# State-space layer and the end of a cross-attention, reordered by halves

## The chip, the cores and the metric

The kernel runs as one program on one core of a Trainium2 chip. The metric is the device time of an execution in microseconds (us). A profile is one execution, recorded instruction by instruction. In it PE is TensorE's matrix multiplication and PEld its weight loads, DVE is VectorE, ACT is ScalarE, POOL is GpSimd and SP issues most transfers. All work of this layer is in 32-bit floating point; the profile records one such matrix product as two MATMUL records and two LDWEIGHTS records, or one of each where the product is a transpose.

## The reference, cut to what matters

Two layers of attention, then feed-forward, work on 128 tokens (two sequences of 64) of width 256. The change lies in the second layer's cross-attention and in the state-space layer behind it.

```
# cross-attention: 16 heads of 16 channels over 1024 context keys and 64 own keys
attn = softmax(einsum('bhnd,bhmd->bhnm', q * scale, k)); out = einsum('bhnm,bhmd->bhnd', attn, v)
x = x + (out.reshape(B, N, C) @ w_proj.T + b_proj)

# state-space layer on xn = rmsnorm(layernorm(x)) * norm_w
z, xBC, dt = split(xn @ in_w.T)                       # 512, 768 and 8 columns
xBC = silu(causal_conv(xBC, conv_w, 4 taps) + conv_b) # per channel
xs, Bm, Cm = xBC[..., :512], xBC[..., 512:640], xBC[..., 640:]
dt = softplus(dt + dt_bias); A = -exp(A_log)
h = h * exp(dt*A) + (dt * xs) (x) Bm;  y = h . Cm     # step over 64 tokens, 8 heads
y = y + D * xs
y = rmsnorm(y * silu(z)) * gnorm_w
out = y @ out_w.T
```

The recurrence is computed as a masked product: for each head, the 128x128 matrix (Cm . Bm) * exp(cumulated dt*A difference) times dt * xs.

## The kernel before

Each engine has its own instruction list, written out by hand, and engines wait for one another by semaphores. `made(name)` is the value of a semaphore at which a named result is there, `tick(name)` the increment at the instruction that makes it; `ONCE` lists them in order. `step(ins)` makes DVE wait for its own instruction. `stay_warm(n, times)` puts 128x128 products of the identity, whose result nobody reads, into PE's list. PSUM has eight banks of 512 columns; `bank(n)` is one, `W[n]` two.

**Cross-attention's end.** A loop over 16 rows (a pair of heads of one sequence each) has PE make scores, DVE their maximum (L1160), ACT the exponentials with sums, PE transposes and products with the values (`attend1`, L1824). DVE copies four rows' products at a time from bank 6 (L1155); the last copy of 512 columns comes after the last row. DVE inverts all 16 sums, spreads them (L1187), PE spreads them over channels (L1840), PE gathers the heads into channel tiles (32 products of 64 columns, L1849), DVE multiplies 256 columns (L1191), PE projects (two products of 256 columns, L1855), DVE adds to x (L1194), normalises, and PE turns xn over (`turn_x`), which ACT copies to `xT` (L612).

**State-space layer.** Channels lie on partitions, tokens in columns: six tiles `CHT` of xBC (four of xs, then B and C). PE makes all six tiles (12 products, L1871), the step size dt (L1875) and z (L1879). DVE and ACT copy xBC to `XP` in SBUF; ACT applies the last tap and the bias for all tiles (L840), DVE the other three taps (18 instructions, L1222). Between the second and third of these rounds stand DVE's three instructions on dt (L1229 to L1231), for which PE's decay products wait (L1893, 8 of them, and L1895 for the sums). Then one tanh over all 768 columns (L847), one product by DVE (L1235), B times C and the transposes of xs (L1898, L1900), DTX and MT over all heads (L1240, L1245), PE's 8 products with them (L1906), DVE's four instructions on y, of 512 columns each (L1253 to L1255 with the D and norm-weight ones ahead), PE's output product (L1912) and sum of squares (L1917), DVE's variance (L1258), POOL's power and DVE's xn (L1260).

Of the kernel before, what the change touches and what calls it, by code (L numbers as in the profile page):

```python
# [6 lines left out]
ALU = mybir.AluOpType  # L7
# [22 lines left out]
CHT = CONV // P  # L30
PAD = NQ + TAPS - 1
# [89 lines left out]
SELF_BANK = ((4, 7), (5, 6))  # L121

# [89 lines left out]
def cut(base, at, *free):  # L212
# [5 lines left out]
    if len(free) == 1:  # L218
# [9 lines left out]
        "q1_ps", "k1_ps", "v1_ps", "rb_ps", "o1T_ps", "out1_ps", "xbc_ps", "dt_ps", "z_ps", "decay_ps", "G_ps",  # L228
        "xs_ps", "ym_ps", "y_tok_ps", "ssq_ps", "sc_ps", "pq_ps", "km_ps", "vm_ps", "lg_ps",
        "scT_ps", "rank_ps", "pmT_ps", "retT_ps", "ret_ps", "gate_ps", "route_ps", "maskT_ps"],  # L230
    "scalar_made": [
        "sqk_ready", "qr_sb", "sqq_ready", "qTA_sb", "kTA_sb", "simA_exp", "ptA_sb", "gT_sb", "xat_dup", "k1_sb", "rb_sb", "expA", "xbc_sbA", "dte",
        "dtl", "z_tanh", "conv_tanh", "cums", "ex_ready", "gm_ready", "ysq_ready", "pq_sb", "sct", "km_sb",
        "vm_sb", "pm_exp", "pmT_sb", "retT_sb", "gate_tanh", "hn_hi", "rz", "maskT_sb"],
    "vector_made": [
        "null_sb", "nv_ready", "kn_ready", "simA_max", "probsA", "hm_ready", "gT_lo", "rsel_ready", "o1_ready", "xbc_sbV",
        "dtn_ready", "dtA_ready", "conv_done", "xs_act", "M_ready", "yg_ready", "ya_ready", "scz", "scb_ready",
# [4 lines left out]
def perceiver_kernel(nc, x_in, ctx_in, ctxT_in, units_in, const_in, cols_in, vecs_in, rows_in, gate_in, out):  # L242
    with ExitStack() as stack:
# [161 lines left out]
        RSEL, RB, OT1 = cut(work, 0, ROWT, 32), cut(work, 512, KT, TOK), cut(work, 768, KT, TOK)  # L405
        probs1 = cut(pbuf, 0, 4, 1152)

        XP, C1 = cut(scr, 0, CHT, B, PAD), cut(scr, 832, CHT, TOK)
        XC, TH = cut(scr, 1600, CHT, TOK), cut(scr, 2368, CHT * TOK)
        ZS, ZT, ZW = cut(scr, 3136, DIN), cut(scr, 3648, DIN), cut(scr, 4160, DIN)  # L410
        DTX, Y2, GM = cut(scr, 4672, DIN), cut(scr, 5184, DIN), cut(scr, 5696, TOK)
        DX = cut(scr, 0, DIN)
        EX, MT = cut(pbuf, 0, NH, TOK), cut(pbuf, 1024, NH, TOK)
        YA, YGT, YSQ = cut(pbuf, 2048, DIN), cut(pbuf, 2560, 4, TOK), cut(scr, 3648, DIN)
# [106 lines left out]
        def _(pool):  # L521
# [23 lines left out]
            for n in range(N_RSQRT):  # L545
# [34 lines left out]
                if n == 6:  # L580
# [9 lines left out]
                    for n, (raw, (lo, hi)) in enumerate(((work, BIAS1), (xn, BIAS2))):  # L590
# [6 lines left out]
                        pool.wait_ge(ev("rows2_split"), n + 1)  # L597
                if n == 7:

                    pool.memset(XP[:, :, :, 0:TAPS - 1], 0.0).then_inc(ev("xp_zero"), 1)  # L600
# [5 lines left out]
        def _(act):  # L606
# [218 lines left out]
            act.wait_ge(*made("rb_ps"))  # L825
            act.copy(RB, bank(1)[:, 0:DIM].rearrange("p (i t) -> p i t", i=KT)).then_inc(*tick("rb_sb"))


            act.activation(expA, v_("A_log"), ACT.Exp).then_inc(*tick("expA"))
# [69 lines left out]
        def _(dve):  # L899
# [317 lines left out]
            for k in range(TAPS - 1):  # L1217
                for t in range(CHT):
                    if k == 0:
                        dve.wait_ge(ev("tap3"), t + 1)  # L1220
# [872 lines left out]
```

## Time and profile before

| | |
|---|---|
| time, median of 3 runs | 482.88 us (482.57 to 483.1) |
| the profiled execution | 483.39 us, span 481.5 us |
| PE busy | 460.1 us of the span, 3634 records |
| DVE, ACT, POOL busy | 263.4, 239.4, 124.5 us |
| granted TensorE clock | 1.000 over the span |
| state-space layer, first product to variance | 384.19 to 405.85 us |

The span runs from the first to the last instruction; the profiled execution's own time lies 1.89 us above it. PE's busy share says little in these two stages, since the identity products count as busy. What releases DVE, ACT and PE at each hand-over is read from the instructions in order of time.

### The profile page before, as it was taken

Reading aid. Unit: us, or ns where it says so; the run is one execution under the profiler, and the core shown is the slowest. Engines: PE = TensorE matmul, PEld = TensorE weight load, DVE = VectorE, ACT = ScalarE, POOL = GpSimd, SP = SyncE. Lnnn points to the kernel's source line nnn. Section 1 sums busy time; section 2 is a strip of 40 time slices with the busy share of each in tenths; the row PEclk is TensorE's granted clock in tenths of the full one; section 3 lists DMA queues with packets and bytes.
Section 4 is the critical chain, followed back from the end, with each engine's and each line's share of the span. In section 5 each row is a group of like instructions: output and inputs, shape, how many; then the busy total and the mean of one; then the engine's idle time right before and its main releaser. Section 6 shows DMA issues by size and latency. Waiting matters only on the chain.

```text
span 481.5 us, 8769 instructions
## 1 busy us (share of the span) xinstructions
PE 460.1 (96%) x3634; PEld 396.0 (82%) x3634; DVE 263.4 (55%) x461; ACT 239.4 (50%) x427; POOL 124.5 (26%) x114
## 2 busy tenths in 40 slices
PE   8999899999999999999978989999999899889997
PEld 7887989899997989899955769996666798778797
DVE  2666223255436231312256898956667465369996
ACT  2567233263535324222035877737888261237772
POOL 1110000002002300000020767969300000008795
PEclk9999999999999999999999999999999999999999
DMA  7925400006100020000079999991000093165000
GB/s 287 385 68 212 175 2 1 1 0 206 58 0 4 10 88 0 2 1 1 0 320 386 338 292 420 389 421 64 2 1 2 12 416 110 78 253 184 0 1 12
DMA packets 13191, 62.66 MB, mean 130 GB/s; under 512 B 1365, under 2 KB 3813, under 8 KB 7392
## 3 DMA queue, kind: packets, MB, share of 16 engines
q1 hardware_dynamic: 11072, 54.31, 29.8%
q0 software_dynamic: 2080, 7.80, 4.6%
q8 instruction: 29, 0.48, 0.4%
q14 instruction: 10, 0.08, 0.1%
HBM read 61.97 MB, written 0.13 MB: 129 GB/s over the span
## 4 chain that ended last, share of the span: by engine, by line
PE 73%; DVE 12%; POOL 6%; ACT 5%; issue 3%; DMA 1%; SPq 0%; DVEq 0%; ACTq 0%; POOLq 0%
PE W L1479 19%; PE W L1435 15%; POOL w_lo L541 5%; PE W L1638 5%; PE W L1708 4%; PE W L1762 3%; PE W L1807 3%; DVE w_lo L942 3%; PE W L1452 3%; PE W L1824 2%; PE W L1358 2%; PE W L1501 2%; DVE acts L1112 2%; PE W L1664 1%; PE W L1387 1%
## 5 line engine op out<-in xcount | busy, mean ns | idle before, releaser
L1479 PE MATMUL W<-probs_turned_hi,ctx_split_hi 128*128 128x256 f32 x256 | 72.9, 285 | 2.5 <-issue 2.5
L1479 PE MATMUL W<-probs_turned_hi,ctx_split_lo 128*128 128x256 f32 x256 | 72.5, 283 | 0.0
L1479 PE MATMUL W<-probs_turned_lo,ctx_split_hi 128*128 128x256 f32 x256 | 72.4, 283 | 0.0
L979 DVE TENSOR_TENSOR probs_turned_lo<-W,probs_turned_hi 128x512 fp32r<-128x512 f32 x32 | 20.6, 687 | 64.9 <-ACT probs_turned_hi L678 64.9
L550 POOL TENSOR_TENSOR small<-small,const 128x1 f32<-128x1 f32 (+2 forms) x10 | 6.9, 691 | 177.4 <-DVE small L1052 75.3
L1479 PEld LDWEIGHTS W<-probs_turned_hi,ctx_split_hi 128*128 128x128 f32 x256 | 49.1, 192 | 3.8 <-issue 3.3
L541 POOL TENSOR_TENSOR w_lo<-arena,w_hi 128x320 fp32r<-128x320 f32 x32 | 43.9, 1386 | 29.2 <-ACT w_hi L619 29.1
L1479 PEld LDWEIGHTS W<-probs_turned_lo,ctx_split_hi 128*128 128x128 f32 x256 | 49.1, 192 | 0.2
L1479 PEld LDWEIGHTS W<-probs_turned_hi,ctx_split_lo 128*128 128x128 f32 x256 | 49.1, 192 | 0.0
L942 DVE TENSOR_TENSOR w_lo<-arena,w_hi 128x704 fp32r<-128x704 f32 (+1 forms) x36 | 44.8, 1280 | 6.0 <-ACT w_hi L619 5.6
L697 ACT ACTIVATE pbuf<-W,small 128x1024 f32<-128x1024 f32 x16 | 17.9, 1117 | 59.6 <-DVE small L999 59.6
L541 POOL TENSOR_TENSOR w_lo<-ctxmem,w_hi 128x320 fp32r<-128x320 f32 (+1 forms) x30 | 46.7, 1579 | 1.9 <-ACT w_hi L619 1.5
L1708 PE MATMUL W<-w_hi,acts 128*128 128x256 f32 x240 | 44.2, 286 | 0.0
L619 ACT CAST w_hi<-arena 128x1024 fp32r<-128x1024 f32 x36 | 37.6, 1050 | 10.5 <-PE W L1638 6.1
L1435 PE MATMUL W<-ctx_turned_hi,q_keys_hi 128*128 128x512 f32 x128 | 41.0, 402 | 0.5 <-DVE q_keys_lo L972 0.5
L1435 PE MATMUL W<-ctx_turned_lo,q_keys_hi 128*128 128x512 f32 x128 | 39.7, 391 | 0.0
L1435 PE MATMUL W<-ctx_turned_hi,q_keys_lo 128*128 128x512 f32 x128 | 39.6, 390 | 0.0
L1708 PEld LDWEIGHTS W<-w_hi,acts 128*128 128x128 f32 x240 | 38.3, 191 | 0.1
L1638 PE MATMUL W<-w_hi,acts 128*128 128x512 f32 x112 | 36.4, 398 | 1.4 <-issue 1.3
L1358 PE MATMUL W<-const 128*128 128x128 f32 x290 | 36.6, 281 | 0.5 <-ACT xT L612 0.5
L1358 PEld LDWEIGHTS W<-const 128*128 128x128 f32 x290 | 34.7, 195 | 2.0 <-ACT xT L612 0.9
L689 ACT COPY scr<-W 128x256 f32<-128x256 f32 x32 | 11.8, 368 | 48.9 <-PE W L1479 48.9
(387 smaller groups left out, 923.0 us busy)
## 6 DMA issues: line engine op xcount, KB each, us to landing
arena<-units_dram SPq DMA_DIRECT2D x22, 1024.0 KB, 11.5
ctxmem<-units_dram SPq DMA_DIRECT2D x16, 1024.0 KB, 13.8
fixed<-units_dram SPq DMA_DIRECT2D x6, 1024.0 KB, 6.1
pbuf<-ctx_dram POOLq DMA_DIRECT2D x4, 512.0 KB, 5.2
ctxmem<-ctxT_dram SPq DMA_DIRECT2D x8, 256.0 KB, 11.3
ctxmem<-ctx_dram SPq DMA_DIRECT2D x2, 1024.0 KB, 14.5
scr<-ctx_dram POOLq DMA_DIRECT2D x3, 512.0 KB, 4.4
vecs<-vectors_dram POOLq DMA_DIRECT2D x1, 1040.0 KB, 7.6
```

What stands on the lines that cost most here:

```text
L541: pool.tensor_tensor(w_slot(1, p)[:, lo:hi], half_in(p)[:, lo:hi], f32(w_slot(0, p)[:, lo:hi]), ALU.subtract).then_inc(ev("lo_by_gpsimd"), 1)
L619: act.copy(w_slot(0, p), half_in(p)).then_inc(ev(hi_done(p)[0]), 1)
L697: act.activation(probs0[:, r % 2, :], W[r % 2][:, :], ACT.Exp, bias=negm[:, r:r + 1], accum_out=stat[:, r, 1:2]).then_inc(ev("exp_done"), 1)
L942: dve.tensor_tensor(w_slot(1, p)[:, lo:hi], half_in(p)[:, lo:hi], f32(w_slot(0, p)[:, lo:hi]), ALU.subtract).then_inc(ev("lo_by_vector"), 1)
L979: dve.tensor_tensor(PT[1][at], bank(4 + c).rearrange("p (t m) -> p t m", t=4), f32(PT[0][at]), ALU.subtract).then_inc(ev("pl_sb"), 1)
L1358: pe.matmul(bank(n)[:, 0:P], ident, ident, start=True, stop=True)
L1435: mm = pe.matmul(W[r % 2][:, kh * 512:(kh + 1) * 512], QP[a][:, c, j, :], CXT[z][:, c, kh * 512:(kh + 1) * 512], start=(c == 0 and n == 0) ...
L1452: mm = pe.transpose(bank(4 + c)[:, t * P:(t + 1) * P], probs0[:, r % 2, (4 * c + t) * P:(4 * c + t + 1) * P], ident)
L1479: mm = pe.matmul(ps, CXN[a][:, t, c * P:(c + 1) * P], PT[z][:, t, :], start=(t == 0 and n == 0), stop=(t == KEYT - 1 and n == 2))
L1638: mm = pe.matmul(bank(4 + hf), XS[a][:, e, k, :], w_slot(z, p)[:, hf * 512:(hf + 1) * 512], start=u == "m1e0" and k == 0 and n == 0, stop= ...
L1708: mm = pe.matmul(bank(n % (E + 1) % 4)[:, 0:DIM], UTS[a][:, t, :], w_slot(z, p)[:, (t % 4) * DIM:(t % 4 + 1) * DIM], start=(t == 0 and i = ...
L1762: mm = pe.matmul(W[r % 2][:, kh * 512:(kh + 1) * 512], QZ[at:at + 32, j // 2, b].rearrange("p h q -> p (h q)"), KEYS[at:at + 32, b, j // 2 ...
```

## The change

The step size goes first: PE makes dt ahead of xBC, ACT takes its exponential and logarithm at once, and DVE's three instructions on dt come after the first three taps. B and C are convolved by PE: ACT builds ten 128x128 diagonal matrices from the taps and the bias of these two tiles, ahead of xT, and PE adds five products for each tile in bank 5. The four tiles of xs are read by DVE straight from PSUM, each in a bank of its own (`RAW_BANK`), in two pairs; tanh, gate, transposes, decays, DTX and MT and the head products go by halves. D is halved once in advance and becomes four diagonal matrices, whose products open the accumulation of y in PSUM. gnorm_w is multiplied into the output matrix by POOL (`wo_scaled`), during the cross-attention. The output product and the sum of squares go by halves, the sum first.

In the cross-attention the sums are inverted and spread in two halves, the first inside the loop (DVE's rows 10 and 12); the last row's product goes to bank 3 and is copied alone, the three before it together; heads are gathered, joined and projected by channel tile, the second tile first. Of the identity products 12, 12, 6, 9, 6 and 7 stood here; now 5, 2 and 5 do. The mask's two products (`neg`, 512 columns each) move ahead of `turn_x`.

```diff
+            for i in range(CHT - XST):
+                for k in range(TAPS):
+                    act.mul(DIAG[:, i, k, :], ident, cw[:, XST + i, k:k + 1])
+                act.mul(DIAG[:, i, TAPS, :], ident, p_("conv_b")[:, XST + i:XST + i + 1])
+            for t in range(XST):
+                ins = act.mul(DIAG_D[:, t, :], ident, p_("D")[:, t:t + 1])
+            ins.then_inc(*tick("diag_ready"))
             keep_xT(bank(0))
...
+            for t in (2, 3):
+                act.wait_ge(ev("raw_ps"), t + 2)
+                act.activation(C1[:, t, :], bank(RAW_BANK[t])[:, 0:TOK], ACT.Identity, bias=p_("conv_b")[:, t:t + 1],
+                               scale=cw[:, t, TAPS - 1:TAPS]).then_inc(ev("tap3"), 1)
+            act.activation(spare, c_("neghalf"), ACT.Exp)
...
+            decays(0)
+            conv_tanh(0)
+            decays(1)
...
+            conv_tanh(1)
...
+                if r == ROWT // 2 + 2:
+                    invert_sums(0)
...
+            for i in (1, 0):
+                join_heads(i)
...
+            first_tap(0)
+            first_tap(1)
+            tap(0, 2, after=1)
+            dve.wait_ge(*made("dtl"))
+            step(dve.tensor_tensor(dt, dtm, dte, ALU.add))
+            step(dve.tensor_tensor(dtAn, dt, expA, ALU.mult))
+            dve.tensor_scalar(dtA, dtAn, -1.0, None, ALU.mult).then_inc(*tick("dtA_ready"))
+            tap(1, 2, after=2)
+            tap(0, 1, after=3)
+            tap(1, 1, after=4)
+            tap(0, 0, after=5)
+            tap(1, 0, after=6)
+            dve.wait_ge(ev("tap3"), 2)
+            tap(2, 2)
+            tap(3, 2)
+            tap(2, 1, after=8)
+            tap(3, 1, after=9)
+            gate_xs(0)
+            tap(2, 0, after=10)
+            tap(3, 0, after=11)
...
+            heads_of(0)
+            heads_of(1)
+            dve.wait_ge(*made("z_tanh"))
             step(dve.scalar_tensor_tensor(out=ZS, in0=ZT, scalar=1.0, in1=bank(4), op0=ALU.add, op1=ALU.mult))
-            dve.wait_ge(*made("xs_ps"))
...
+            for i in range(CHT - XST):
+                dst = bank(5)[:, i * P:(i + 1) * P]
+                pe.matmul(dst, DIAG[:, i, TAPS, :], c_("ones"), start=True, stop=False)
+                for k in range(TAPS):
+                    mm = pe.matmul(dst, DIAG[:, i, k, :], XP[:, i, :, k:k + NQ], start=False, stop=(k == TAPS - 1))
+            mm.then_inc(*tick("conv45_ps"))
```

In the order of the instructions this is seen at three places. On PE, at the front of the state-space layer, the list before runs as follows: xBC (L1871), dt (L1875), z (L1879), the mask (L1889), identity products (L1358), decays and their sums (L1893, L1895).

```order
L1871 MATMUL W<-xT,arena 128x128 x12
L1875 MATMUL W<-arena,xT 128x8 x2
L1879 MATMUL W<-xT,arena 128x128 x8
L1889 MATMUL W<-const 128x512 x2
L1358 MATMUL W<-const 128x128 x12
L1893 MATMUL W<-const,small 128x128 x8
L1895 MATMUL W<-small,const 128x8
```

And this is PE's list of the change at the same place: dt (L1980), xBC (L1985), the sums and decays (L1994, L1996), bias and taps of B and C (L2007, L2009), transposes of xs (L2015), half of z (L2021).

```order
L1980 MATMUL W<-arena,xT 128x8 x2
L1985 MATMUL W<-xT,arena 128x128 x12
L1994 MATMUL W<-small,const 128x8
L1996 MATMUL W<-const,small 128x128 x8
L2007 MATMUL W<-const,pbuf 128x128
L2009 MATMUL W<-scr,pbuf 128x128 x4
L2007 MATMUL W<-const,pbuf 128x128
L2009 MATMUL W<-scr,pbuf 128x128 x4
L2015 MATMUL W<-const,scr 128x128 x2
L2021 MATMUL W<-xT,arena 128x128 x4
```

The decays move ahead of z, ten products of the convolution come in, and the identity products between are gone. On ACT, from the exponential of A_log (`small<-vecs`) on, the list before is this, with the dt exponential at L837, the last tap of the convolution at L840, and the logarithm at L843:

```order
L829 ACTIVATE small<-vecs 128x8
L612 COPY xT<-W 128x256
L832 COPY scr<-W 128x4x64
L837 ACTIVATE small<-small 128x8
L840 ACTIVATE scr<-scr,cols 128x128 x6
L843 ACT_TABLE_LOAD
L843 ACTIVATE small<-small 128x8
L845 ACT_TABLE_LOAD
L845 ACTIVATE scr<-W 128x512
```

This is the same stretch of ACT's list in the change; L846, L847 and L849 build the diagonals, L853 and L855 are exponential and logarithm of dt, L859 the last tap of two tiles, L861 an exponential whose result nobody reads.

```order
L842 ACTIVATE small<-vecs 128x8
L846 ACTIVATE pbuf<-const,cols 128x128 x4
L847 ACTIVATE pbuf<-const,cols 128x128
L846 ACTIVATE pbuf<-const,cols 128x128 x4
L847 ACTIVATE pbuf<-const,cols 128x128
L849 ACTIVATE pbuf<-const,cols 128x128 x4
L624 COPY xT<-W 128x256
L853 ACTIVATE small<-small 128x8
L855 ACT_TABLE_LOAD
L855 ACTIVATE small<-small 128x8
L859 ACTIVATE scr<-W,cols 128x128 x2
L861 ACT_TABLE_LOAD
```

Fourteen diagonals now stand ahead of the copy of xT, and nothing stands between dt's exponential and the load for its logarithm. At the end of the layer PE's list before has the head products (L1906), the output (L1912) and the squares (L1917):

```order
L1906 MATMUL W<-pbuf,scr 64x128 x8
L1358 MATMUL W<-const 128x128 x6
L1912 MATMUL W<-arena,pbuf 128x256 x4
L1917 MATMUL W<-const,scr 128x1 x4
L1358 MATMUL W<-const 128x128 x7
```

In the change D's products (L2033) come ahead of the head products (L2039), and output (L2045) and squares (L2049) alternate:

```order
L2033 MATMUL W<-scr,pbuf 128x128 x4
L2039 MATMUL W<-pbuf,scr 64x128 x8
L1459 MATMUL W<-const 128x128 x2
L2045 MATMUL W<-arena,pbuf 128x256 x2
L2049 MATMUL W<-const,scr 128x1 x2
L2045 MATMUL W<-arena,pbuf 128x256
L2049 MATMUL W<-const,scr 128x1 x2
L2045 MATMUL W<-arena,pbuf 128x256
```

The squares' last product moves ahead of the output's last.

## Rows read from the trace of the kernel before

**Rows 1.** Busy time of each engine in the state-space layer (windows).

```profile
core 0: us, PE busy (x) PEld busy (x) DVE busy (x) ACT busy (x) POOL busy (x), PEclk, DMA share, GB/s
384.20:405.90 21.70, 21.44 (x172) 19.50 (x173) 13.77 (x36) 10.13 (x24) 0.00 (x0) 1.00 0.71 291
```

**Rows 2.** Timeline, cross-attention's end: start, us, engine line, out<-in [idle before <-releaser].

```profile
375.81 0.64 PE L1824 MATMUL W<-scr,ctxmem 128*32 128x128 f32 x16
...
376.70 0.69 DVE L1155 COPY ctxmem<-W 128x512 f32<-128x512 f32 x1 [1.20 <-PE W L1824]
...
377.44 1.10 PE L1849 MATMUL W<-ctxmem,const 128*32 128x64 f32 x64 [0.34 <-DVE ctxmem L1155]
...
378.68 0.42 DVE L1191 TENSOR_TENSOR work<-W,work 128x256 f32<-128x256 f32 x1 [1.29 <-PE W L1849]
...
379.16 1.13 PE L1855 MATMUL W<-arena,work 128*128 128x256 f32 x4 [0.62 <-DVE work L1191]
...
380.33 0.42 DVE L1194 TENSOR_TENSOR x<-W,x 128x256 f32<-128x256 f32 x1 [1.22 <-PE W L1855]
...
383.76 0.37 ACT L612 COPY xT<-W 128x256 f32<-128x256 f32 x1 [6.09 <-PE W L1374]
```

**Rows 3.** The chain in order of time, PE's pieces in the state-space layer: start, us, what.

```profile
384.19 2.94 PE W L1871 x24
...
393.78 2.05 PE W L1893 x16
...
397.70 0.45 PE W L1900 x4
```

**Rows 4.** Timeline, front of the state-space layer, DVE and ACT.

```profile
387.83 0.15 DVE L1212 TENSOR_TENSOR small<-W,vecs 128x8 f32<-128x8 f32 x1
...
388.63 2.40 ACT L840 ACTIVATE scr<-scr,cols 128x128 f32<-128x128 f32 x6
...
391.05 1.28 ACT L843 ACT_TABLE_LOAD   x1
392.35 0.21 ACT L843 ACTIVATE small<-small 128x8 f32<-128x8 f32 x1
...
393.15 0.17 DVE L1229 TENSOR_TENSOR small<-small 128x8 f32<-128x8 f32 x1
...
393.63 1.66 DVE L1222 SCALAR_TENSOR_TENSOR scr<-scr,cols 128x128 f32<-128x128 f32 x6
...
396.26 2.18 ACT L852 ACTIVATE pbuf<-W,small 128x128 f32<-128x128 f32 x8
```

**Rows 5.** Timeline, second half of the state-space layer.

```profile
398.25 0.69 DVE L1240 SCALAR_TENSOR_TENSOR scr<-W,small 128x512 f32<-128x512 f32 x1 [0.49 <-PE W L1900]
...
398.98 1.23 DVE L1245 TENSOR_TENSOR pbuf<-pbuf,scr 128x1024 f32<-128x1024 f32 x1
...
400.25 1.09 PE L1906 MATMUL W<-pbuf,scr 128*64 128x128 f32 x16
...
403.03 1.99 PE L1912 MATMUL W<-arena,pbuf 128*128 128x256 f32 x8
...
404.65 1.08 PEld L1917 LDWEIGHTS W<-const,scr 128*128 128x128 f32 x8
...
405.85 0.16 DVE L1258 TENSOR_SCALAR small<-W 128x1 f32<-128x1 f32 x1 [2.27 <-PE W L1917]
...
406.67 0.48 DVE L1260 TENSOR_SCALAR xn<-W,small 128x256 f32<-128x256 f32 x1 [0.66 <-POOL small L550]
```

**Rows 6.** Timeline, DVE in the attention loop, row 11's maximum.

```profile
358.28 1.23 DVE L1160 TENSOR_REDUCE small<-W 128x1 f32<-128x1024 f32 x1 [0.38 <-PE W L1762]
```

**Rows 7.** Timeline of POOL: first cast for the experts, last of 1024 columns, next power.

```profile
321.12 1.04 POOL L537 CAST w_hi<-ctxmem 128x1024 fp32r<-128x1024 f32 x1 [0.66 <-DMA ctxmem<-units_dram]
...
332.47 2.36 POOL L541 TENSOR_TENSOR w_lo<-ctxmem,w_hi 128x1024 fp32r<-128x1024 f32 x1
...
381.95 0.82 POOL L550 TENSOR_TENSOR small<-small,const 128x2 f32<-128x2 f32 x1 [40.94 <-DVE small L919]
```

**Rows 8.** Timeline of ACT in an earlier layer, a scale per partition, from SBUF.

```profile
262.48 1.86 ACT L760 ACTIVATE acts<-xT,small 128x128 fp32r<-128x128 f32 x6 [1.38 <-DVE small L1104]
```

More of the change, by code:

```diff
@@ new lines, in _, with decays, conv_tanh @@
+            act.wait_ge(*made("cums"))
+            def decays(hf):
+                act.wait_ge(*made(f"decay{hf}_ps"))
+                for h in range(4 * hf, 4 * hf + 4):
+                    ex = act.activation(EX[:, h, :], W[1][:, h * TOK:(h + 1) * TOK], ACT.Exp, bias=cums[:, h:h + 1])
+                ex.then_inc(*tick(f"ex{hf}_ready"))
+            def conv_tanh(pair):
+                act.wait_ge(ev("conv_done"), pair + 1)
+                act.activation(TH[:, 2 * pair:2 * pair + 2, :], C1[:, 2 * pair:2 * pair + 2, :], ACT.Tanh, scale=0.5)\
+                    .then_inc(ev("conv_tanh"), 1)
@@ L857, in _ @@
[L857 removed]
+            for hf in range(2):
+                act.wait_ge(*made(f"ya{hf}_ready"))
+                act.activation(YSQ[:, 2 * hf:2 * hf + 2, :], YA[:, 2 * hf:2 * hf + 2, :], ACT.Square)\
+                    .then_inc(*tick(f"ysq{hf}_ready"))
             keep_xT(bank(0))
@@ new lines, in _, with turn_xs @@
+            pe.wait_ge(*made("diag_ready"))
+            pe.wait_ge(*made("xp_sb"))
+            for i in range(CHT - XST):
[4 more added lines that the diff above has]
+            mm.then_inc(*tick("conv45_ps"))
+            def turn_xs(pair):
+                pe.wait_ge(*made(f"xc{pair}"))
+                for n in range(2):
+                    mm = pe.transpose(bank(XS_BANK[pair])[:, n * P:(n + 1) * P], XC[:, 2 * pair + n, :], ident)
+                mm.then_inc(*tick(f"xs{pair}_ps"))
@@ new lines, in gates @@
+            def gates(tiles):
+                for t in tiles:
+                    for k in range(KT):
+                        mm = pe.matmul(bank(4)[:, t * P:(t + 1) * P], wz[:, k, t * P:(t + 1) * P], xT[:, k, :],
+                                       start=(k == 0), stop=(k == KT - 1))
+                return mm
+            turn_xs(0)
+            pe.wait_ge(*made("cums"))
+            gates((0, 1))
+            pe.wait_ge(*made("xc45"))
+            pe.matmul(bank(5)[:, 2 * P:3 * P], XC[:, 4, :], XC[:, 5, :], start=True, stop=True).then_inc(*tick("G_ps"))
@@ new lines, in _ @@
+            turn_xs(1)
+            gates((2, 3)).then_inc(*tick("z_ps"))
+            for t in range(XST):
+                pe.matmul(bank(YM_BANK[t // 2])[:, (t % 2) * P:(t % 2 + 1) * P], DIAG_D[:, t, :], XC[:, t, :],
+                          start=(t % 2 == 0), stop=False, skip_group_check=True)
+            for pair in range(2):
+                pe.wait_ge(*made(f"M{pair}_ready"))
+                for h in range(4 * pair, 4 * pair + 4):
+                    o, at = HD * (h % 2), (h % 4) // 2 * P
+                    mm = pe.matmul(bank(YM_BANK[pair])[o:o + HD, at:at + P], DTX[:, h * HD:(h + 1) * HD], MT[:, h, :],
+                                   start=False, stop=True, skip_group_check=True)
+                mm.then_inc(*tick(f"ym{pair}_ps"))
@@ new lines, in _, with mixed, squares @@
+            pe.wait_ge(ev("wo_scaled"), 1)
+            def mixed(t):
+                return pe.matmul(bank(2)[:, 0:DIM], YA[:, t, :], wo2[:, t, :], start=(t == 0), stop=(t == XST - 1))
+            def squares(tiles):
+                for t in tiles:
+                    mm = pe.matmul(bank(1)[:, 0:1], YSQ[:, t, :], c_("ones")[:, 0:1], start=(t == 0), stop=(t == XST - 1))
+                return mm
+            stay_warm(3, 2)
+            pe.wait_ge(*made("ya0_ready"))
+            mixed(0)
```

321 lines of the change are left out of this document (165 added, 156 removed).

## The prediction

> **What bounds the kernel now.** I first read the windows over the state-space layer. PE is busy 21.44 of 21.70 us at the full clock [rows 1], but 33 of its products there are idle ones of the identity, so that share names no bound. The chain of waits follows PE through these idle products as well, so I used it only for what a run of real products costs, and read the hand-overs from the timeline: at each instruction, what it waited for and how long. The reader is to see two stretches in which one instruction at a time works.
>
> At the attention's end [rows 2]: the last row's products, a copy of 512 columns, the gather, one DVE product, the projection, the addition. From the copy at 376.70 to the addition at 380.33 nothing overlaps.
>
> In the state-space layer, from PE's first product at 384.19 [rows 3] to the variance at 405.85, 21.66 us pass. The order is at fault: DVE has dt's sum only at 387.83, behind all of xBC; ACT does six taps (2.40 us) before it loads the table for the logarithm at 391.05; DVE gets to dt's last three instructions at 393.15, between its taps, and PE's decays start at 393.78 [rows 3, 4]. Then come tanh and gate over everything, and DVE's instructions over 512 and 1024 columns, one behind the other with PE between them [rows 5].
>
> **Prices.** PE: 12 products of 128x128 in 2.94 us, eight in 2.05 with the last one's way out [rows 3], so 0.235 each; a transpose 0.11 (four in 0.45); a product of 256 columns 0.41 (four from 403.03 to 404.65); a sum of squares 0.25 a tile (four in 1.08 of weight loads); a half of the head products 0.52 (eight in 1.09 with the way out) [rows 5]. A result is with its reader some 0.2 after PE could go on. DVE: 0.69 for 512 columns and 0.42 for 256 [rows 2, 5], hence 0.285 for 128; a tap 0.277 (six in 1.66) [rows 4]. ACT: 0.27 for a decay (eight in 2.18), 0.21 for a small one, 1.28 for a table load [rows 4]. A hop from engine to engine: 0.05 between L1155's end and L1849, 0.14 into L1191 [rows 2].
>
> **Attention's end.** The last copy shrinks from 0.69 to 0.285, so the gather starts at 377.04 and not at 377.44. It has the same columns in half as many products: 1.10 less 0.25 for the way out, halved, is 0.43 a tile. The second tile's result is there at 377.72, DVE multiplies it from 377.86 to 378.15; the first tile's is gathered to 377.90 and multiplied to about 378.58. PE projects the second tile in the meantime and the first from 378.7; with 0.45 and 0.2 the addition starts at 379.37: **0.96 saved**. If each of the three new hand-overs costs 0.14 more, 0.5; if the joins overlap fully, 1.2.
>
> What must stay hidden here: the first half of the sums (two DVE instructions of about 0.2) enters the loop ahead of row 11's maximum, which had 0.38 to spare [rows 6]; 0.1 at most is left over, once, and ACT and PE have other rows' work. Halving D is one small instruction (0.15 [rows 4]) ahead of DVE's wait for the queries. Uncovered, the two cost 0.3 us together. Behind `turn_x` the mask's two products and five idle ones take at most eight plus five times 0.235, 3.06, from about 379.17: 382.23, against 382.33 when xn is there. If the cover is missing by 0.2, 0.2 is lost.
>
> POOL's scaling of the output matrix is 1024 columns, 2.36 us; POOL idles 40.94 us before its power at 381.95, and the matrix was issued on SP ahead of the expert unit that POOL already had at 321.12 [rows 7]. Uncovered it would delay xn by 2.4 us.
>
> **Diagonals on ACT.** Fourteen instructions with a scale per partition. The nearest row below is L852 with 0.27, the one above L840 with 2.40/6 = 0.40, which has a pointer for scale and for bias [rows 4]. I take 0.31, from L760, six in 1.86 with a scale alone [rows 8], as here. That is 4.3 us from about 377.6 (after the two copies of RB), so 381.9; PE offers xT at 383.76 - 0.96 = 382.8 [rows 2]. At 0.40 it ends at 383.2 and 0.4 us is lost.
>
> **State-space layer**, in us from PE's first product. *Step size:* dt's two products are done by 0.47, DVE starts at 0.67, three instructions 0.2 apart and a hop bring ACT's exponential to 1.35; load and logarithm 1.28 + 0.21 give 3.1, DVE's three instructions and hops 3.86. PE has xBC ready at 0.47 + 2.82 = 3.3 and waits 0.55. Before, the same point lay at 393.78 - 384.19 = 9.59.
>
> *PE from there:* sums 0.22, decays 1.88, B and C 10 x 0.235 = 2.35 (8.31), two transposes 0.22 (8.53), half of z 0.94 (9.47), a wait of 0.09 for the gated B and C, their product 0.235, a wait of 0.13 for the second pair, transposes 0.22, z 0.94 (11.1), D 0.94 (12.04), heads 1.04 (13.08), two idle ones 0.47, two output products 0.82, squares 0.5, output 0.41, squares 0.5: 15.77, at DVE 15.97. Before 21.66: **5.69 saved**. POOL's power and xn follow as before, and the last output product ends earlier than the power.
>
> *Whether ACT and DVE keep up:* ACT has the logarithm at 3.1, two taps to 4.0, a second load to 5.3 (for the exponential), four decays to 6.8, tanh of the first pair (0.4) 7.2, four decays 8.25, tanh of B and C at 8.56 to 9.0, of the second pair 9.35. DVE does five taps after 3.86 to 5.2 and four to 6.3, gates the first pair 7.25 to 7.67 (PE wants it at 8.31), two taps to 8.25, gates B and C 9.1 to 9.5 and the second pair to 9.9, then DTX 0.42 and MT 0.69 for either half: 10.95 and 12.0, and PE wants them at 12.04 and 12.56. So DVE has 0.6 us of room before its first gate and 0.5 at the end. Taps read PSUM now, which no row of a tap shows: below 0.277, as from SBUF, above 0.42, as 256 columns from PSUM in L1191 [rows 2]; at 0.42 the first gate comes 0.4 later and still fits.
>
> **Sum.** 0.96 + 5.69 = 6.65 of the profiled 483.39 is 476.74; this execution stood 0.51 above the median, so 476.23. Some ten hops on this path were put at 0.05, and the rows show up to 0.14; a quarter of a microsecond for them gives **476.5**. Behind the layer everything shifts together: transfers for the experts are issued at the same two hand-overs, which come earlier, and from 424 us on the view of waits has no engine waiting for a transfer.
>
> **Rivals.** (1) *The middle becomes a ping-pong.* Between the convolution's end at 8.31 and the heads at 12.04 PE and DVE hand over eight times, and DVE's own work (gates 0.84, DTX 0.84, MT 1.38) fills 3.1 of 3.7 us. For it: the room is 0.5 us. Against: no instruction there needs two foreign results at once. If each hand-over costs 0.14 and DVE's room is gone, M and ZS come 0.7 later each: 476.5 + 1.4 = 477.9. Chance 0.17.
>
> (2) *A table load stalls ACT beyond its 1.28.* Both loads are on the path's edge: the first delays dt directly, the second the first tanh. Were each 1.38 longer, dt would cost 1.38, and the second load the same less 0.6 us of room: 2.1, hence 478.6. Against it: the logarithm starts at 392.35, 0.02 behind the load's end [rows 4]. Chance 0.04. The Trainium skill, "ScalarE: Activation LUTs", section "What ACT_TABLE_LOAD costs", gives 1283 ns for a load and some 1380 ns of draining with it; the load agrees with the trace's 1.28, the draining does not show in that row.
>
> (3) *The other sign: the array's clock drops.* With 31 identity products fewer ahead of the variance, PE's pieces would run at 1.2 instead of 2.4 GHz. They make up some 14.5 us of the new layer, so each microsecond of them at half clock adds one; from 6.4 us on the kernel is slower, and with all of it 491. Against: the clock was 1.00 here [rows 1], and PE's waits in the new order sum to about 1 us of 16. Chance 0.02. The Trainium skill, "TensorE: Matmul & The Clock Gate", Part 1, says that a half-rate clock is the default and activity releases it; no row of this trace shows it at work.
>
> (4) *The gain doesn't last:* the experts wait for weights. Then 482.9. Against: see the sum. Chance 0.02.
>
> (5) *More than forecast:* joins overlap fully and the waits of PE vanish: 1.2 + 6.2 saved, 475.4. Chance 0.07.
>
> **How the numbers follow.** The forecast has 0.68, with 475.7 to 477.3 as its own range: the low end is half of what (5) adds, the high end the late diagonals (0.4) and three slow hand-overs (0.4). To hold 8 in 10 the range takes in (5) and most of (1): 475.4 to 478.3. What a measurement of this kernel can tell from no change is about 0.2%, 1 us. Faster: forecast, (1), (2), (5), 0.96; within: (4), 0.02; slower: (3), 0.02.
>
> **What would show it.** In the new profile: the addition to x some 1 us earlier; ACT's last diagonal before PE's turn of xn; decays starting 3.9 us behind PE's first product; the convolution's ten products in 2.4; the variance 16.0 behind the first product; a clock of 1.00. The prediction is wrong if ACT reaches xT late, if the load for the logarithm starts later than dt's exponential, or if DVE's MT of the second half ends after 12.6 us.

## The result and the profile after

The changed kernel takes 475.55 us (median of 4 runs, 473.9 to 477.58) where the kernel before takes 482.82 (482.57 to 483.1, run in the same comparison): a ratio of 0.9846, 95% interval 0.981 to 0.9883. The forecast was 476.5 us, from 475.4 to 478.3. The direction and the mechanism held, but the gain is larger: 7.27 us where 6.38 were forecast. The median lies 0.95 us below the forecast, at the low edge of its range; taken by the ratio, 0.9846 of 482.82 is 475.38, just beyond that edge. Executions more than 1.5% above the fastest of the same kernel are left out of this and all later ratios, though not of the medians.

The attention's end in the timeline of the changed kernel, which answers to [rows 2]:

```profile
375.20 0.64 PE L1926 MATMUL W<-scr,ctxmem 128*32 128x128 f32 x16
...
376.10 0.29 DVE L1221 COPY ctxmem<-W 128x128 f32<-128x128 f32 x1
...
376.44 1.08 PE L1946 MATMUL W<-ctxmem,const 128*32 128x128 f32 x32
...
377.22 0.73 DVE L1204 TENSOR_TENSOR hn<-W,xn 128x128 f32<-128x128 f32 x2 [0.83 <-PE W L1946]
...
378.74 0.43 DVE L1257 TENSOR_TENSOR x<-W,x 128x256 f32<-128x256 f32 x1 [0.79 <-PE W L1963]
...
379.77 1.27 ACT L849 ACTIVATE pbuf<-const,cols 128x128 f32<-128x128 f32 x4
...
382.18 0.37 ACT L624 COPY xT<-W 128x256 f32<-128x256 f32 x1 [1.13 <-PE W L1475]
```

From the last row's products to the addition to x it takes 378.74 - 375.20 = 3.54 us, before 4.52. The last four diagonals are done at 381.04, and ACT then waits 1.13 us for the turned xn: they lie off the path.

The state-space layer, first as windows of the changed kernel (against [rows 1]), then its timeline (against [rows 3] to [rows 5]):

```profile
core 0: us, PE busy (x) PEld busy (x) DVE busy (x) ACT busy (x) POOL busy (x), PEclk, DMA share, GB/s
382.60:398.30 15.70, 15.35 (x132) 14.64 (x133) 10.02 (x33) 8.61 (x22) 0.00 (x0) 1.00 0.97 397
```

```profile
382.60 0.61 PE L1980 MATMUL W<-arena,xT 128*128 128x8 f32 x4 [0.46 <-ACT xT L624]
...
383.93 0.21 ACT L853 ACTIVATE small<-small 128x8 f32<-128x8 f32 x1 [1.38 <-DVE small L1273]
384.15 1.28 ACT L855 ACT_TABLE_LOAD   x1
...
385.45 0.21 ACT L855 ACTIVATE small<-small 128x8 f32<-128x8 f32 x1
...
386.34 0.39 PE L1994 MATMUL W<-small,const 128*128 128x8 f32 x2 [0.35 <-DVE small L1315]
386.50 1.28 ACT L861 ACT_TABLE_LOAD   x1
386.59 2.03 PE L1996 MATMUL W<-const,small 128*128 128x128 f32 x16
...
388.45 0.39 PE L2007 MATMUL W<-const,pbuf 128*128 128x128 f32 x2
...
389.56 0.43 DVE L1306 SCALAR_TENSOR_TENSOR scr<-scr 128x256 f32<-128x256 f32 x1 [0.99 <-ACT scr L874]
...
390.69 0.38 PE L2015 MATMUL W<-const,scr 128*128 128x128 f32 x2
...
390.91 1.06 PE L2021 MATMUL W<-xT,arena 128*128 128x128 f32 x8
...
391.80 0.47 PE L2029 MATMUL W<-scr 128*128 128x128 f32 x2
...
393.31 0.68 DVE L1345 TENSOR_TENSOR pbuf<-pbuf,W 128x512 f32<-128x512 f32 x1
...
394.27 1.09 PE L2039 MATMUL W<-pbuf,scr 128*64 128x128 f32 x16
...
395.84 1.03 PE L2045 MATMUL W<-arena,pbuf 128*128 128x256 f32 x4
...
398.13 0.16 DVE L1359 TENSOR_SCALAR small<-W 128x1 f32<-128x1 f32 x1 [2.29 <-PE W L2049]
```

From PE's first product to the variance it is 398.13 - 382.60 = 15.53 us, before 21.66. The sums of the decays start 386.34 - 382.60 = 3.74 us behind the first product; before, the decays stood at 9.59. PE's rows carry one bracket behind the first, 0.35 us for dtA at 386.34; the later products follow one another without a releaser. DVE and ACT carry brackets of a microsecond in the same stretch (0.99 ahead of the first gate). That is what a stage looks like whose bound has moved to PE.

The sum of the two stages is 0.98 + 6.13 = 7.11 us. The two spans differ by 481.5 - 473.7 = 7.8 us; the rest lies elsewhere. In the opening, whose instructions are the same in both kernels, ACT's L664 starts at 10.47 us here and the same instruction at 11.05 before. This lead of 0.6 us is still there at the attention's end, where 375.20 stands against 375.81. Behind ACT's next copy of xT (400.00) come 73.70 us, before 73.76.

### The profile page after: what moved, and what is told of

It reads as the page before. It is cut to its first block, busy times and chain, and to the rows that moved or that the text cites. A ratio compares the mean times of both kernels' runs of the same rounds, so it can differ in the third digit from the quotient of the medians.

```text
span 473.7 us, 8586 instructions
## 1 busy us (share of the span) xinstructions
PE 453.6 (96%) x3534; PEld 389.4 (82%) x3534; DVE 260.8 (55%) x464; ACT 242.0 (51%) x440; POOL 126.7 (27%) x115
## 4 chain that ended last, share of the span: by engine, by line
PE 74%; DVE 11%; POOL 6%; ACT 6%; issue 3%; DVEq 0%; ACTq 0%; POOLq 0%
PE W L1580 20%; PE W L1536 15%; POOL w_lo L549 5%; PE W L1739 5%; PE W L1809 4%; PE W L1863 4%; PE W L1908 3%; DVE w_lo L974 3%; PE W L1553 3%; PE W L1926 2%; PE W L1602 2%; DVE acts L1144 2%; PE W L1459 1%; PE W L1765 1%; PE W L1488 1%
## 5 line engine op out<-in xcount | busy, mean ns | idle before, releaser
L974 DVE TENSOR_TENSOR w_lo<-ctxmem,w_hi 128x704 fp32r<-128x704 f32 x26 | 34.3, 1368 | 0.2
L1809 PE MATMUL W<-w_lo,acts 128*128 128x256 f32 x120 | 33.9, 283 | 0.0
```

The source lines that it names most:

```text
L974: dve.tensor_tensor(w_slot(1, p)[:, lo:hi], half_in(p)[:, lo:hi], f32(w_slot(0, p)[:, lo:hi]), ALU.subtract).then_inc(ev("lo_by_vector"), 1)
L1809: mm = pe.matmul(bank(n % (E + 1) % 4)[:, 0:DIM], UTS[a][:, t, :], w_slot(z, p)[:, (t % 4) * DIM:(t % 4 + 1) * DIM], start=(t == 0 and i = ...
```

## The experiments

All runs name the stretch from PE's first product of the layer to the variance, since it came out alike in both traces of the changed kernel (15.53 us), while whole times of one kernel scatter by some microseconds. "Time" is the median, with the ratio to the kernel before, run in the same comparison. Where one time is given, it is that of the profiled execution alone.

**The changed kernel again.** No edit.

> The changed kernel once more, nothing altered. Theory: what the change itself gives is 0.99 us at the attention's end and 6.13 us between PE's first product of the state-space layer and the variance; both stretches are computed by the same instructions each time, so they come out at 15.5 us (first product to variance) within 0.1 us again. The other 0.6 us of the first comparison lay in the opening, before 19 us, where the instructions of both kernels are the same, and will be anywhere from 0 to 0.6 us here. Rival: the layer's stretch itself varies by a microsecond from execution to execution, and explains the scatter of 473.9 to 477.6 us. Expected time 475.5 us, from 474 to 477.5 us.

First product to variance was 15.53 us, last row's products to addition 3.53, the rest behind the layer 73.73. Time 474.8 us, ratio 0.9821 (0.9769 to 0.9872). The profiled execution itself took 482.38 us and shows where the scatter arises: not in the layer. In its opening ACT's L664 starts at 11.04 us, as in the kernel before and 0.57 later than in the first run of the same code. And in the first layer's experts PE waits for weights, as the timeline (ACT, which casts the weights as they arrive, then PE) and the windows of this run show:

```profile
298.49 1.99 ACT L631 CAST w_hi<-arena 128x1024 fp32r<-128x1024 f32 x2 [4.87 <-DMA arena<-units_dram]
...
301.27 0.58 PE L1809 MATMUL W<-w_hi,acts 128*128 128x256 f32 x1 [3.91 <-DVE w_lo L974]
```

```profile
288.00:297.00 9.00, 8.52 (x64) 7.68 (x63) 5.12 (x7) 4.16 (x6) 3.17 (x2) 1.00 1.07 324
297.00:301.00 4.00, 0.36 (x4) 0.16 (x2) 1.37 (x1) 2.07 (x3) 1.31 (x2) 0.92 1.02 420
301.00:307.00 6.00, 5.73 (x27) 5.73 (x28) 4.82 (x6) 3.11 (x4) 4.78 (x4) 0.50 1.02 423
307.00:312.00 5.00, 5.00 (x43) 5.00 (x43) 4.71 (x6) 3.59 (x4) 2.76 (x3) 0.98 1.02 423
```

After a wait of 3.91 us the granted clock stands at 0.50 (1.2 GHz) from 301 to 307 us although PE works, and comes back to 0.98. Against the first run, this execution is 0.57 us late at 11 us and 6.88 us late at the last row's products (382.08 instead of 375.20). The theory held for these two traces, and the rival (the layer itself varies) fell.

**The attention's end alone**, in the kernel before.

```diff
+                if r == ROWT + 3:
+                    dve.wait_ge(ev("pv1_ps"), ROWT)
+                    dve.tensor_copy(PV[:, ROWT - 1, :], bank(3)[:, 0:P]).then_inc(ev("pv1_sb"), 1)
...
+            for i in (1, 0):
+                join_heads(i)
...
+            for i in (1, 0):
+                gather_heads(i)
```

> The kernel before with the attention's end of the change alone (halved sums, the last row in a bank of its own, gather, join and projection by channel tile); the state-space layer as before. Theory: the addition to x comes 1.0 us earlier against the last row's products, the layer still takes 21.7 us, and the time is 481.9 us against 482.9. Rival: the idle identity products behind the projection or the turning of xn take the gain back, and the time is 482.7 us or more.

Last row's products to addition 3.53 us, addition to first product 3.86 as in every kernel here, the layer 21.66 as before. Time 482.39 us, ratio 0.9978 (0.9946 to 1.001): the whole time alone does not settle a gain of 0.2%, the stretch of 0.99 us does. In this run's opening the clock was 0.51 from 8 to 11.5 us.

**The step size late**, in the changed kernel.

```diff
-            for k in range(KT):
-                mm = pe.matmul(bank(4)[:, 0:NH], xT[:, k, :], wd[:, k, :], start=(k == 0), stop=(k == KT - 1))
-            mm.then_inc(*tick("dt_ps"))
...
                 raw(t, bank(RAW_BANK[t])[:, 0:P]).then_inc(ev("raw_ps"), 1)
+            for k in range(KT):
+                mm = pe.matmul(bank(4)[:, 0:NH], xT[:, k, :], wd[:, k, :], start=(k == 0), stop=(k == KT - 1))
+            mm.then_inc(*tick("dt_ps"))
```

> The changed kernel with the step size made behind all of xBC on PE, and DVE's four instructions on it behind the first three taps; all else as in the change. Theory (the step size opens a chain in which PE is then the bound): dt comes 12 products of 0.235 us later, 2.8 us, and everything behind it moves with it; first product to variance 18.3 us instead of 15.5, time 478.3 us. Rival (the gain comes from fewer and smaller instructions on DVE and ACT, and DVE's taps would hold PE up in any case): at most 1 us is lost, 16.5 us and 476.5 us.

First product to variance 20.94 us: 5.41 lost, where the theory said 2.8 and the rival at most 1. Time 480.82 us, ratio 0.9944 (0.9909 to 0.9978); the mean granted clock of each of the ten executions lies between 0.989 and 0.996. The timeline of PE in this run, and its windows:

```profile
387.63 0.51 PE L1990 MATMUL W<-arena,xT 128*128 128x8 f32 x4
391.25 0.60 PE L1994 MATMUL W<-small,const 128*128 128x8 f32 x2 [3.10 <-DVE small L1315]
391.69 3.76 PE L1996 MATMUL W<-const,small 128*128 128x128 f32 x16
```

```profile
388.00:390.40 2.40, 0.14 (x2) 0.05 (x1) 0.59 (x4) 1.58 (x3) 0.00 (x0) 0.97 0.97 410
390.40:397.00 6.60, 5.75 (x27) 5.76 (x28) 3.72 (x15) 4.94 (x15) 0.00 (x0) 0.50 1.03 433
397.00:406.00 9.00, 9.00 (x79) 8.48 (x79) 4.32 (x10) 2.07 (x5) 0.00 (x0) 1.00 0.43 179
```

PE's sums start 391.25 - 384.85 = 6.40 us behind the first product instead of 3.74, 2.66 later: the theory's term. From there to the variance it takes 14.54 us instead of 11.79: another 2.75, and in this stretch the eight decays take 3.76 us instead of 2.03, at a clock of 0.50.

**The step size late, and PE kept busy.** The next run separates the two terms.

```diff
             pe.wait_ge(*made("dtn_ready"))
+            stay_warm(4, 9)
             pe.wait_ge(*made("dtA_ready"))
```

> The kernel with the late step size, and nine idle products of the identity in the wait that it opens on PE (behind DVE's reading of dt, so that about 0.9 us of the 3.1 us stay idle, and all nine end before dtA is there). Nothing is computed sooner by them. Theory: of the 5.41 us that the late step size cost, 2.66 are the later dt, and 2.75 come from the clock, which was granted at half from 390.4 to 397 us, behind PE's wait of 3.1 us. With PE busy in the wait the clock stays at 1.00, and first product to variance is 18.2 us instead of 20.94. Rival: the late dt itself costs the 5.4 us, by DVE's and ACT's order, and the stretch stays at 20.9 us.

18.18 us, the clock 1.00 throughout the layer, and over the whole execution in three of four. Time 477.72 us, ratio 0.9901 (0.9866 to 0.9937). Nine products whose result nobody reads make the layer 2.76 us faster. The late step size itself costs 2.65.

**No idle products**, in the changed kernel: `stay_warm` with 5, 2 and 5 taken out.

```diff
-            stay_warm(6, 5)
...
-            stay_warm(3, 2)
...
-            stay_warm(3, 5)
```

> The changed kernel without any of its 12 idle products of the identity in this part (five ahead of the turning of xn, two ahead of the output product, five ahead of the second turning). Theory: PE's longest wait is then some 1.3 us, the clock stays at 1.00 throughout, and only the two on the path are gained, 0.2 us: first product to variance 15.3 us. Rival (the idle products hold the clock up): the granted clock falls to 0.50 behind the turning of xn or of the layer's output, and several microseconds are lost, each microsecond of products at half clock adding one.

16.39 us, 0.86 lost, and another 4.24 in what follows the layer (77.94 us behind the copy of xT instead of 73.70). Time 477.25 us, ratio 0.9889 (0.9825 to 0.9954). The timeline of PE in this run, and its windows:

```profile
382.24 0.33 PE L1472 MATMUL W<-const,xn 128*128 128x128 f32 x1 [1.27 <-DVE xn L1266]
...
383.60 4.38 PE L1984 MATMUL W<-xT,arena 128*128 128x128 f32 x24
...
400.89 0.33 PE L1472 MATMUL W<-const,xn 128*128 128x128 f32 x1 [0.86 <-DVE xn L1361]
```

```profile
380.00:385.00 5.00, 3.27 (x21) 2.19 (x19) 2.90 (x13) 2.46 (x9) 0.95 (x2) 0.98 0.20 62
385.00:388.00 3.00, 3.00 (x16) 3.00 (x16) 2.28 (x10) 1.64 (x3) 0.00 (x0) 0.50 1.01 418
389.00:401.00 12.00, 10.89 (x94) 9.95 (x93) 6.62 (x18) 5.47 (x17) 0.65 (x2) 1.00 0.86 361
402.00:410.00 8.00, 8.00 (x27) 5.98 (x28) 0.67 (x4) 1.10 (x4) 0.00 (x0) 0.50 0.35 134
```

In this execution the theory fell and the rival held. PE waited 1.27 us for xn and 0.46 for xT, then worked, and the clock fell to 0.50 while it worked, from 385 to 388; twelve xBC products took 4.38 us instead of 2.92. The 0.2 us of the two products on the path was gained as expected (heads to output product 1.35 us apart instead of 1.57) and is inside the 0.86. Behind the layer the same happened for at least 8 us. But this did not come each time: of the four executions, two have a mean granted clock of 1.000 and took 475.04 and 474.64 us, no longer than the change, and two, with 0.986 and 0.989, took 481.09 (the one profiled) and 479.47. So without the idle products the clock fell in some executions and not in others; what decides it stays open.

**More on PE and more on DVE**, two runs with one instruction group added to the changed kernel.

```diff
             pe.wait_ge(*made("cums"))
+            stay_warm(4, 4)
             gates((0, 1))
```

> The changed kernel with four idle products of the identity put into PE's list ahead of the first half of z. Theory (PE's list is the bound in the middle of the layer): four times 0.223 us, less the 0.2 us that PE waits behind them: first product to variance 16.2 us, 0.7 to 0.9 more than 15.53. Rival (DVE and ACT set the middle): at most 0.3 us more, 15.8 us.

```diff
+            dve.tensor_copy(XP[:, :, :, TAPS - 1:], C1[:, 0:2, :].rearrange("p t (b q) -> p t b q", b=B))
             heads_of(0)
             heads_of(1)
```

> The changed kernel with one more instruction of 256 columns on DVE, whose result nobody uses, ahead of the first half of DTX. Theory: DVE has 0.5 us and more of room ahead of the heads, and the 0.4 us are hidden: first product to variance 15.53 us, at most 0.1 more. Rival (DVE is as tight as PE): 0.42 us more, 15.95 us.

PE's four products took 0.89 us and made the stretch 16.26 us, 0.73 more; the other 0.16 us were mostly short waits of PE in the change, below what a bracket shows (from B times C to the second pair's transposes it takes 0.32 us there and 0.23 here). Times are 476.29 and 475.77 us. DVE's instruction made it 15.52 us, no more than without it. It took 0.29 us and not 0.42, and DVE's second MT ended only 0.12 us later, so this shows less room than intended. Both agree with PE as the bound in the middle.

**B and C on DVE and ACT again**, in the changed kernel: the ten products with diagonals replaced by two taps of ACT and six of DVE.

```diff
+            for k, after in ((2, None), (1, 12), (0, 14)):
+                for t in (4, 5):
...
+                    ins = dve.scalar_tensor_tensor(out=c1, in0=XP[:, t - XST, :, k:k + NQ], scalar=cw[:, t, k:k + 1], in1=c1,
+                                                   op0=ALU.mult, op1=ALU.add)
```

> The changed kernel with B and C convolved by ACT and DVE as before (two taps with bias on ACT, six instructions on DVE, after the gate of the first half), instead of ten products of PE with diagonals. Theory (PE's ten products cost 2.23 us of its list, but buy more on the other engines): DVE's six taps of 0.28 and ACT's two of 0.45 come ahead of B's and C's gate, PE waits for it and for the second half behind it; first product to variance 17.0 us, 16.5 to 17.5. Rival (PE's list alone is the bound, so that shorter is faster): 15.5 us or less.

17.63 us, 2.10 more; time 476.74 us. PE's list is 2.24 us shorter, and PE waits 2.20 us for the first gate, as the timeline of this run shows; behind that wait eight records of z take 1.76 us instead of 1.06, at a granted clock of 0.50 from 391 to 393 us. These records of z cost nothing on the path, since PE then waits another 0.45 us for the gate of B and C, which DVE makes. But from there to D's products it takes 394.46 - 392.37 = 2.09 us instead of 1.48. Without this 0.61 the stretch would be 17.0 us, an estimate from these rows, and the value expected. The theory held: here DVE and ACT set the middle, and PE's shorter list gains nothing.

```profile
389.89 0.44 PE L2018 MATMUL W<-const,scr 128*128 128x128 f32 x2 [2.20 <-DVE scr L1306]
390.17 1.76 PE L2024 MATMUL W<-xT,arena 128*128 128x128 f32 x8
392.37 0.80 PE L2032 MATMUL W<-scr 128*128 128x128 f32 x2 [0.45 <-DVE scr L1343]
...
394.46 1.06 PE L2036 MATMUL W<-scr,pbuf 128*128 128x128 f32 x8
```

**The four tiles of xs together**, in the changed kernel.

```diff
-                act.wait_ge(ev("conv_done"), pair + 1)
+                act.wait_ge(ev("conv_done"), 2)
...
             decays(0)
+            decays(1)
             conv_tanh(0)
-            decays(1)
...
-            gate_xs(0)
             tap(2, 0, after=10)
             tap(3, 0, after=11)
+            gate_xs(0)
```

> The changed kernel with the four tiles of xs finished together: both tanh and both gates wait for the taps of all four tiles (all decays stand ahead of the first tanh on ACT). PE's list is as in the change. Theory: the first gate comes some 1.5 us later and PE, which has nothing else in front of it, waits for it about 1.0 us; first product to variance 16.5 us. Rival (the halves are worth nothing, as DVE and ACT catch up): 15.6 us.

15.82 us, 0.29 more, against 1.0 expected; time 476.74 us. The first gate stands 391.58 - 383.59 = 7.99 us behind the first product instead of 6.96, 1.03 later. What it waits for is not the taps, which are all done at 390.06, but ACT's tanh, which in this edit stands behind all eight decays:

```profile
387.18 2.88 DVE L1295 SCALAR_TENSOR_TENSOR scr<-W,cols,scr 128x126 f32<-128x126 f32 x11
...
391.08 0.47 ACT L874 ACTIVATE scr<-scr 128x256 f32<-128x256 f32 x1
391.58 0.42 DVE L1306 SCALAR_TENSOR_TENSOR scr<-scr 128x256 f32<-128x256 f32 x1 [1.52 <-ACT scr L874]
```

PE had room for most of that: its turning of xs starts 0.38 us later (392.06 - 383.59 against 390.69 - 382.60). Finishing xs in halves, with the tanh between the decays, is thus worth 0.29 us; that the taps alone cost anything is not shown.

**No spare exponential**, in the changed kernel.

```diff
-            act.activation(spare, c_("neghalf"), ACT.Exp)
```

> The changed kernel without the spare exponential behind the logarithm, which loads the table for the decays ahead of them. Theory: the load of 1.28 us then starts only when the first four decays are there, some 1.2 us later than now; ACT's first tanh comes 0.9 us later, of which PE has 0.5 us in hand: first product to variance 15.9 us, 15.8 to 16.3. Rival (a table load stalls ACT for longer than its own 1.28 us): another 1.4 us, 17.3 us.

16.11 us, 0.58 more; time 474.89 us. ACT loads the table behind the decays' arrival. Against PE's first product, the first gate starts 1.02 us later, the turning of xs 0.37 and B times C 0.56. The load took 1.28 us (from 386.61), and the first exponential started at 387.90, 0.01 behind its end: no stall beyond.

**The gap filled**, in the changed kernel, with `stay_warm(3, 2)` left out.

```diff
+            pe.wait_ge(*made("diag_ready"))
+            pe.wait_ge(*made("xp_sb"))
+            pe.matmul(bank(5)[:, 0:P], DIAG[:, 0, TAPS, :], c_("ones"), start=True, stop=False)
+            pe.matmul(bank(5)[:, 0:P], DIAG[:, 0, 0, :], XP[:, 0, :, 0:NQ], start=False, stop=False)
             pe.wait_ge(*made("dtA_ready"))
...
-            stay_warm(3, 2)
```

> The changed kernel with the first two of PE's ten products for B and C (the bias and the oldest tap of the first tile) moved ahead of PE's wait for the decays' input, into the 0.5 us in which PE idles there, and without the two idle identity products ahead of the output product. Theory (PE's list is the bound from the decays to the heads): 0.45 us for the two products and 0.2 us for the idle ones, first product to variance 14.9 us, time 474.9 us. Rival (DVE and ACT are as tight as PE in the middle): PE only waits longer for the gated xs, C and B or for M, and no more than the 0.2 us is gained, 15.3 us.

14.95 us, 0.58 less than the change, as expected, and the clock 1.00 in the whole layer. The timeline of PE in this run has no bracket left at the place:

```profile
385.14 0.39 PE L1995 MATMUL W<-const,pbuf 128*128 128x128 f32 x2
385.37 0.39 PE L1996 MATMUL W<-scr,pbuf 128*128 128x128 f32 x2
385.65 0.39 PE L1998 MATMUL W<-small,const 128*128 128x8 f32 x2
```

Time 474.31 us (473.31 to 475.72), ratio 0.9813 (0.9766 to 0.986), beside 474.8 and 0.9821 for the change in the same comparison: the difference of whole times lies within their scatter, that of the stretch does not. By its stretch this is the best version found.

**Both sums ahead of three output products**, on top of the filled gap.

```diff
             mixed(0)
-            mixed(1)
             pe.wait_ge(*made("ysq0_ready"))
             squares((0, 1))
-            pe.wait_ge(*made("ya1_ready"))
-            mixed(2)
             pe.wait_ge(*made("ysq1_ready"))
             squares((2, 3)).then_inc(*tick("ssq_ps"))
+            mixed(1)
+            mixed(2)
             mixed(3).then_inc(*tick("y_tok_ps"))
```

> The kernel with the filled gap, and behind the heads the two sums of squares ahead of the last three output products (one product, both sums, three products) instead of in halves. Theory: the variance comes 0.8 us earlier, PE's output products then end some 0.4 us after it would be wanted and set the end: ACT's copy of the turned xn behind the layer comes 0.4 to 0.5 us earlier than with the filled gap, 16.3 us behind PE's first product against 16.82 there, 17.40 in the change and 23.55 before; time 0.4 us below that of the filled gap. Rival (the sums then wait for ACT's squares, and PE idles): no gain.

The variance stands at 14.07 us, 0.88 earlier, but ACT's copy of xT behind the layer at 16.81 us, against 16.82 with the filled gap: nothing is gained. Time 476.06 us, ratio 0.98 (0.9746 to 0.9854). DVE's xn waits 1.32 us for the output products and comes 0.22 us earlier than with the filled gap, but the five idle products start only behind the output products and hold PE until 400.65 us, when the turning of xn starts; xn was complete at 400.29. The rival named this outcome but not this way: the sums follow the first output product without a wait for the squares.

## Where the prediction held, and which step failed

The direction, the order and the causes held; the sizes did not, and nearly all on one side. The two stages were to give 0.96 + 5.69 us less a quarter of a microsecond, 6.40, and gave 7.11. The step that failed is the size of the layer's term: "5.69 saved", less the quarter for ten hops, is 5.44, and the layer gave 6.13, 0.69 more. Of these, 0.25 are the hops, 0.12 the step size, and 0.32 PE's list behind it, priced at "0.235 each" and with a wait that did not come. Besides, the scatter of executions stood at nothing, and 0.6 us of the profiled difference come from it.

- **Attention's end, 0.96 predicted, 0.98 measured.** The gather begins 0.39 us earlier against the last row (0.40 predicted), because the copy ahead of it takes 0.29 us instead of 0.69, and from the gather to the addition it takes 2.30 us (2.33 predicted). The end alone gives the same 0.99 without the rest.
- **The layer, 15.97 predicted, 15.53 measured.** The order was right: step size, a short wait of PE, then PE's list. The sizes: dtA reaches PE at 3.74 us and not 3.86, with a wait of 0.35 and not 0.55. From there it takes 11.79 us, not 12.11: the convolution 2.24 (2.35 predicted), each half of z 0.89 (0.94), the wait of 0.09 ahead of B times C does not appear, and from the first output product to the variance it takes 2.29 (2.43). Against this, D took 0.99 (0.94), and the heads with two idle products 1.57 (1.51).
- **"So 0.235 each".** This price takes 0.12 us off the twelve products of [rows 3] for the last one's way out, and 0.17 off the eight. The difference of the two rows, four products in 2.94 - 2.05 = 0.89 us, gives 0.223, and that is what the products of the convolution and of z take (and the four idle ones, 0.89, in the run with more on PE). The eight decays stayed near the price, 1.86 us or 0.233 each.
- **"A quarter of a microsecond for" ten hops** was not needed: without it the sum, 6.65, is still 0.46 below the 7.11 of the two stages. On a path that PE sets, hand-overs between the other engines are covered, as far as the run with more on DVE shows.
- **The position of the profiled execution.** The prediction subtracted 0.51 for the profiled execution and gave the scatter of executions no term. The opening alone set the two profiled executions 0.6 us further apart in favour of the change, in code that the change does not touch. This part is luck: in the second trace of the changed kernel the same instruction starts at 11.04 us, as before. Later runs of the kernel before ranged from 481.02 to 489.23 us. So of the 1.44 us between the profiled 475.55 and the 476.99 that the sum gave for it, 0.44 is the layer's price, 0.25 the hops, 0.6 the opening, and the last 0.15 the attention's end and small remainders.
- **What no run takes apart.** From the heads' first product to the first output product 1.57 us pass, before 403.03 - 400.25 = 2.78, and from there to the variance 2.29, before 2.82. D's diagonals, gnorm_w in the output matrix and the output by halves changed there together; how much each gives is not shown.
- **Rival 1, the ping-pong,** did not come: DVE's second MT ends 393.99, before PE reaches its half of the heads, and one more instruction on DVE cost nothing. That instruction delayed the second MT by only 0.12 us, so the room is shown to that extent.
- **Rival 2, the table loads:** the logarithm starts 0.02 us behind the load's end here too, and taking the second load's place away cost 0.58, not 1.4 more. The Trainium skill, "ScalarE: Activation LUTs", section "What ACT_TABLE_LOAD costs", has the 1283 ns right for this trace; its drain of some 1380 ns shows in none of these rows.
- **Rival 3, the clock,** did not come in the change but was the nearest danger, and the 0.02 given to it rested on a weak argument, that PE's waits sum to little. Three of the runs with an edit had it in their traces: behind a wait of 3.10 us, behind a wait of 2.20 us, and, when the idle products were gone, behind waits of 1.27 and 0.46 us (there the clock fell in two executions of four). The Trainium skill, "TensorE: Matmul & The Clock Gate", Part 1, says that half rate is the default and activity lifts it. These runs agree, with 0.50 granted behind each of these stretches and 1.00 again some microseconds later, while PE works. The clock was an open cost: no bracket of PE in [rows 2 to 5] is above 0.62 us, since idle products stood in the longer waits, and the longest wait of PE in that whole trace is 1.4 us, with the clock at 1.00; so it could not show what a longer one costs.
- **Rival 4, the experts waiting:** 73.70 us behind the layer against 73.76. It fell.
- **Rival 5, more than forecast,** is nearest in number: 475.4, or 475.5 when its own 1.2 + 6.2 are taken off 482.88. Its mechanism did not come: the attention's end gave 0.98 and not 1.2, and PE still waits 0.35 us for dtA and about 0.1 ahead of the second pair's transposes. That the profiled time stands there is in part the luck of the opening.

## What to carry to other kernels

When a chain of hand-overs is rearranged, find which engine's list is without gaps afterwards, price it by a run without gaps and leave the hops of the other engines out; then fill the wait that is left with the next work that does not depend on it. Idle products in a wait are part of the schedule: count how long PE would be idle without them before they are taken out, and try it in several executions, since the clock need not fall in each. Compare a stage by its own stretch in two traces and look at the stretches that the change does not touch first, since those can move the whole time by as much as the change.

## What the runs showed that was not expected

The granted clock fell to 0.50 not only behind a long wait but also while PE was already at full work. In the run without idle products this was some 2 us behind the waits of 1.27 and 0.46 us, for 3 us, and at 402 us, right behind waits of 0.86 and 0.46, for at least 8. Behind the wait of 3.10 us it stayed for 6.6 us, behind one of 3.91 for about 6. One late transfer therefore costs more than its wait: in the second profile of the changed kernel 6.88 - 0.57 = 6.3 us were lost between the opening and the attention's end, and the longest wait of PE was 3.9. A lower clock is no speciality of the changed kernel: in the first comparison of the experiments nine of 23 executions of the kernel before have a mean granted clock of 0.996 or less, with a median of 484.98 us; the other fourteen have 0.999 or 1.000, with a median of 482.96. Why the weights come late in some executions and the opening's transfers vary by up to 0.9 us (ACT's L659 at 8.17 and at 9.07 us with the same code) stays open.
